# Queries' sum of squares in two rounded products, and the last denominators moved behind the second weight matrices

## The chip, the cores and the metric

One core of one Trainium2 chip runs the whole program. The metric is the device time of one execution in microseconds. The engines are TensorE (PE: matmuls and transposes; PEld: its weight loads), VectorE (DVE), ScalarE (ACT), GpSimd (POOL) and SyncE (SP), which issues the DMAs. Matrix results land in PSUM, in banks of 128 partitions x 512 floats; everything else lies in SBUF.

## The reference, cut to what matters

The block is a cross attention of latents on a context, then a self attention in fp8, then a gated attention, each with a residual. The change touches the first.

```python
# x (16, 64, 256), ctx (16, 1601, 128); Wq (256, 2048), Wk, Wv (128, 2048), Wo (2048, 256); 16 heads of 128
def rmsnorm(x, g, eps=EPS):
    var = jnp.mean(jnp.square(x), axis=-1, keepdims=True)
    return x * jax.lax.rsqrt(var + eps) * g
q = (hidden_states @ Wq).reshape(B, Sq, H, D)      # hidden_states = layernorm(x)
k = (encoder_hidden_states @ Wk).reshape(B, Skv, H, D)
v = (encoder_hidden_states @ Wv).reshape(B, Skv, H, D)
q = rmsnorm(q, gq); k = rmsnorm(k, gk)
scores = jnp.einsum('bqhd,bkhd->bhqk', q, k) * scale
out = jnp.einsum('bhqk,bkhd->bqhd', softmax(scores), v)
return out.reshape(B, Sq, H * D) @ Wo
```

## The kernel before

Products in float32 take several passes of TensorE. The kernel avoids most of them: it rounds an operand to a shorter float (type F32R, a "high" part, written by ScalarE), keeps the rest in a "low" part (a subtraction on VectorE or GpSimd), and adds two or three products of rounded parts in PSUM. Each engine has its own list of instructions, written out by hand; semaphores order them. `wait_ge(S.name, n)` holds an engine's queue until the counter has reached n, and `.then_inc` counts when an instruction is done.

**`queries`** (the first stage) computes the normed queries, multiplied by the keys' weights. There are 32 items, a head and one of two groups of 512 latents each. Every engine runs `step(n, m, o)` with m = n - 1 and o = n - 2, so three items are under way. For an item TensorE makes six rounded products into psK (L391, `Wq` times the normed latents), ScalarE squares the result (L459) and rounds it scaled into qgh (L468), VectorE makes the rest qgl (L551). For item m TensorE sums the squares over the 128 partitions: one float32 product with a matrix of ones into psS (L399). ScalarE takes the logarithm (L476), then for item o the exponential y (L464) and its square half (L473); VectorE refines the inverse root in two steps, scaled (L548) and root (L555, both operands in SBUF), and writes the queries from psO, times root (L560). psO comes from three more products (L406). psK, psS and psO have two banks each, square and y two buffers, qgh and qgl three. In items 4, 8, 12 and 16 TensorE also makes Gram matrices of the keys' weights, in items 17, 19, 21 and 23 it turns weights of a later stage, and at `GAIN_AT` and `GAIN_ALL_AT` it reduces a gain. `Wq` is loaded in four pieces; GpSimd makes their low parts wql (L311) and then sets `T.raw` to zero (L314), where three of the pieces lay. SP waits for that and loads the first two batches of the context there (`load_context`, L180, L181), and waits for them (L198) before the stage can end.

**`cross_attention`** runs over 8 pairs of batches, 26 tiles of context rows a pair, 13 a batch, and a pipelined step for each tile. TensorE: a transpose (L850), four key chunks (L808, L809), two halves of scores (L819), two halves of weighing (L828). VectorE: key products (L1238, L1249), the split cTl of the transposed context (L1277), scores scaled (L1260). ScalarE: sums, exponentials, roundings. GpSimd: the softmax sums c_acc and small root steps. A batch's softmax denominators are made while the next batch runs, in two halves of 512 columns. `SUMMED_AT = (0, 3)` gives the tile of the next batch in which TensorE makes each half's sum in the bank psM (L839, L840, in `denominators`); `LOG_AT = (1, 4)` and `INVERSE_AT = (2, 5)` are those of ScalarE's logarithm and exponential; `NEWTON_AT = (2, 5)` and `FULL_AT = (3, 6)` those of VectorE's `newton_start` (L1434, reads psM, counts dneg) and `newton_end` (L1439, two operands in SBUF, counts dfull); `NORM_AT = (5, 7)` that of GpSimd's scaling of the output (L1510). psM is one bank, so the second half's product must wait until the first half's sum has been read; it waits for dneg. In a step VectorE comes to the newton steps last, after `products`, `scale_scores` and `products_summed(i, x, 1)`; TensorE comes to `denominators` after key chunk 1 of the step. `batch_done(i, batch, 2, half)` is the count when `half` halves of this batch are done. The last batch's denominators lie in `end`, with a bank of their own (psT) for the second half.

**`end`** of `cross_attention` multiplies `Wv` and `Wo` of each head into one matrix (`turn` transposes, L888; `matrices`, L904; four heads at a time) and the weighted context with it (`product`, L922, in eight segments of four items). ScalarE and VectorE split the operands (`weighed_high` L1128, `weighed_low` L1320, `v_low` L1310), and again the order is written out by hand. Segments 2 and 3 and the last two need the second half of the latents, whose last batch is scaled by the last denominators.

Of the kernel before, what the change touches and what calls it, by code (L numbers as in the profile page):

```python
# [175 lines left out]
def load_context(nc, sp, T, dram, i, b, sems):  # L176
# [13 lines left out]
             "gram gramh graml zeroed context m8 m2 sel causal iota selb wgate wqkv turn turned gT gtop gall")  # L190
Q_SLOTS = 3
X_SLOTS = 2 * BANK // DIM
ITEM_SEMS = "q square qgh qgl total log y half newton root qw out"


def queries(nc, T, psum, dram):
    psT, psK, psS, psO, psM = psum
    with ExitStack() as ctx:  # L198
# [9 lines left out]
        wk, wq_last = T.queries[:, NPAIR - 1, :, :, :].rearrange("p b h q -> p (b h q)"), sb("wq", [P, WC, BANK])  # L208
# [5 lines left out]
        square, log, half = sb("square", [P, 2, BANK]), sb("log", [P, BANK]), sb("half", [P, BANK])  # L214
        y, scaled, root = sb("y", [P, 2, BANK]), sb("scaled", [P, BANK]), sb("root", [P, BANK])
# [15 lines left out]
        def wq(q):  # L231

            size = WC * BANK
            return wq_last[:, :, :] if q == KC - 1 else T.raw[:, q * size:(q + 1) * size].rearrange("p (k n) -> p k n", k=WC)
# [18 lines left out]
        GAIN_AT, GAIN_ALL_AT = 28, 30  # L253
# [10 lines left out]
        @block.sync  # L264
        def _(sp):
            sp.dma_start(T.xs[:, :, :], dram["x"].rearrange("b q c -> (b q) c").rearrange("(n p) c -> p n c", p=P)).then_inc(S.x, 16)
            for q, sem in enumerate(wq_there):
                sp.dma_start(wq(q), dram["L0_xattn_Wq"].rearrange("(k p) n -> p k n", p=P)[:, :, quad(q)]).then_inc(sem, 16)
# [6 lines left out]
            sp.wait_ge(S.zeroed, 1)  # L275
            for b in range(2):
                load_context(nc, sp, T, dram, 0, b, (S.context, S.context))
            sp.wait_ge(S.context, 64)

        @block.gpsimd  # L280
        def _(pool):
# [27 lines left out]
            for q in range(KC):  # L309
                pool.wait_ge(S.wqh, q + 1)  # L310
                nc.gpsimd.tensor_tensor(wql[:, :, quad(q)], wq(q), wqh[:, :, quad(q)].bitcast(F32), ALU.subtract).then_inc(S.wql, 1)  # L311

            pool.wait_ge(S.wql, KC)
            nc.gpsimd.memset(T.raw[:, :], 0.0).then_inc(S.zeroed, 1)  # L314

        @block.tensor
        def _(pe):
# [51 lines left out]
            def step(n, m, o):  # L369
# [12 lines left out]
                if n is not None:  # L382
                    h, g = items[n]
                    if h % HB == 0 and g == 0:
                        pe.wait_ge(S.wql, h // HB + 1)
# [26 lines left out]
        def _(act):  # L412
            nc.scalar.preload_act_table_set(LN_EXP)

            def wq_high(q):
                act.wait_ge(wq_there[q], 16)
                nc.scalar.activation(wqh[:, :, quad(q)], wq(q), ACT.Copy).then_inc(S.wqh, 1)
# [34 lines left out]
            act.wait_ge(S.made, 1)  # L452

            def step(n, m, o):
# [19 lines left out]
                if m is not None:  # L474
                    act.wait_ge(S.total, m + 1)
                    nc.scalar.activation(log[:, :], psS[:, m % 2, :], ACT.Ln, scale=1.0 / D, bias=T.eps[:, :]).then_inc(S.log, 1)  # L476
# [9 lines left out]
        def _(dve):  # L486
# [44 lines left out]

            def gram_low(q):
# [3 lines left out]
            def step(n, m, o):  # L536
# [7 lines left out]
                if o is not None:  # L544
                    dve.wait_ge(S.half, o + 1)
                    if o:
                        dve.wait_ge(S.root, o)
                    nc.vector.scalar_tensor_tensor(scaled[:, :], psS[:, o % 2, :], float(D * EPS), half[:, :], ALU.add, ALU.mult).then_inc(S.newton, 1)  # L548
# [4 lines left out]
                if o is not None:  # L553
                    dve.wait_ge(S.newton, o + 1)
                    nc.vector.scalar_tensor_tensor(root[:, :], scaled[:, :], 1.5, y[:, o % 2, :], ALU.subtract, ALU.mult).then_inc(S.root, 1)  # L555
                    dve.wait_ge(S.root, o + 1)
                    dve.wait_ge(S.qw, o + 1)
                    if o == GROUPS * (H - HB):
                        dve.wait_ge(S.turned, 2 * WC)
                    nc.vector.scalar_tensor_tensor(out(o), psO[:, o % 2, :].rearrange("p (m q) -> p m q", q=SQ), -1.0,  # L560
# [25 lines left out]
def cross_attention(nc, T, psum, dram):  # L586
    psT, psK, psS, psO, psM = psum
    with ExitStack() as ctx:
# [206 lines left out]
        def _(pe):  # L795
# [35 lines left out]
            def denominators(i, batch, half):  # L831
# [4 lines left out]
                if den_bank(i, batch, half) is psM_all:  # L836
                    pe.wait_ge(S.dneg, batch_done(i, batch, 2, half))
# [39 lines left out]
            def turn(q):  # L877
# [5 lines left out]
                if q >= 2:  # L883
                    pe.wait_ge(S.dneg, batch_done(LAST, 1, 2))
# [120 lines left out]
        def _(act):  # L1005
# [151 lines left out]
            def end(i, batch):  # L1157
                weighed_high(0)
                logarithms(i, batch, 0)
                weighed_high(1)  # L1160
                inverses(i, batch, 0)
                weighed_high(2)
                logarithms(i, batch, 1)
                weighed_high(3)
# [64 lines left out]
        def _(dve):  # L1229
# [150 lines left out]
            def end(i, batch):  # L1380
                weighed_low(0)
                newton_start(i, batch, 0)
                weighed_low(1)
                newton_end(i, batch, 0)
                weighed_low(2)
                newton_start(i, batch, 1)
                weighed_low(3)
                newton_end(i, batch, 1)
                product_low(1)
                next_segment(0)  # L1390
                wo_low(2)
                v_low(2)
                next_segment(1)
# [759 lines left out]
```

## Time and profile before

| | us |
|---|---|
| device time, median of 3 runs | 1481.54 (1479.16 to 1481.94) |
| the profiled execution, its own time | 1480.01 |
| its span (first to last instruction) | 1478.0 |
| TensorE busy | 1386.3 (94%) |
| VectorE busy | 1259.4 (85%) |
| ScalarE busy | 1202.5 (81%) |
| GpSimd busy | 982.6 (66%) |

`queries` runs from 22.7 us (its first product) to 139.5 us, the pipelined steps of `cross_attention` to 1237 us, its end to 1318 us, the two self attentions to the end. A busy time counts an instruction from start to end; matmuls follow each other before the one ahead has ended, so the distance between starts is what one costs. The granted clock is a share of TensorE's 2.4 GHz: 1.00, or 0.50 for 1.2 GHz.

### The profile page before, as it was taken

The page shows a single profiled execution, that of the slowest core. Times are in us where ns is not written, and L with a number is a line of the kernel's source. Part 1 is how long each engine was busy: PE and PEld are TensorE (multiplying, and loading weights), DVE is VectorE, ACT ScalarE, POOL GpSimd, SP SyncE. Part 2 cuts the span into 40 slices and gives each one's busy share as a digit, 9 for nine tenths or more (in the row PEclk, how much of TensorE's full clock was granted, in tenths as well). Part 3 has the DMA queues.
Part 4 walks back from the last instruction along what each step waited for, and adds up shares of the span by engine and source line. Part 5 has one row for each costly group of instructions (what it writes and reads, how often), then busy time and mean ns, then how long its engine had stood idle before and what let it go on. Part 6 is the DMA issues. An engine that isn't in the chain of part 4 may idle for free. (4 is left out here: it accounts for less than half of the span.)

```text
span 1478.0 us, 31543 instructions
## 1 busy us (share of the span) xinstructions
PE 1386.3 (94%) x5980; PEld 936.6 (63%) x5980; DVE 1259.4 (85%) x5006; ACT 1202.5 (81%) x4843; POOL 982.6 (66%) x1505
## 2 busy tenths in 40 slices
PE   5997999999999999999999999999999999966886
PEld 4664666666666666666666666666666666854554
DVE  6776888998989898889989898998998998756985
ACT  5886889898898989898988988898989887535763
POOL 4000788888989898889889898988888885010000
PEclk9998999999999999999999999999999999986998
DMA  4000000000000000000000000000000001000000
GB/s 143 38 1 1 1 2 24 4 21 16 10 23 1 24 1 23 2 23 2 23 13 13 23 1 25 1 23 2 23 1 27 22 30 64 1 1 1 8 7 16
DMA packets 9849, 25.30 MB, mean 17 GB/s; under 512 B 736, under 2 KB 6016, under 8 KB 9520
## 3 DMA queue, kind: packets, MB, share of 16 engines
q1 hardware_dynamic: 9648, 23.49, 4.4%
q14 instruction: 181, 1.48, 0.3%
q8 instruction: 20, 0.33, 0.1%
HBM read 22.44 MB, written 1.05 MB: 16 GB/s over the span
## 5 line engine op out<-in xcount | busy, mean ns | idle before, releaser
L1014 ACT ACTIVATE c_unused<-c_prod 124x128 f32<-124x128 f32 x1664 | 493.1, 298 | 83.6 <-DVE c_prod L1238 77.5
L1554 POOL TENSOR_TENSOR c_acc<-c_acc,c_prob 123x1024 f32<-123x1024 f32 (+1 forms) x192 | 461.9, 2406 | 23.9 <-ACT c_prob L1021 23.2
L1249 DVE CUSTOM_DVE_ANT_0 c_multiplied<-psK,c_c 124x128 f32<-124x128 f32 x1664 | 381.5, 285 | 57.0 <-PE psK L809 57.0
L808 PE MATMUL psK<-wkh,c_cTh 128*124 128x512 f32 x832 | 413.5, 497 | 10.9 <-DVE c_cTl L1277 9.2
L828 PE MATMUL psO<-c_prob,raw 123*128 123x512 f32 (+1 forms) x832 | 392.1, 594 | 0.0
L1238 DVE TENSOR_TENSOR c_prod<-psK,c_c 124x512 f32<-124x512 f32 x416 | 286.0, 688 | 53.4 <-PE psK L809 40.1
L809 PE MATMUL psK<-wkl,c_cTh 128*124 128x512 f32 x832 | 329.6, 396 | 0.0
L1014 ACT ACTIVATION_READ_ACCUMULATOR c_unused<-c_prod 124x1 f32 x1664 | 311.3, 187 | 0.0
L1260 DVE TENSOR_TENSOR c_prob<-psS,c_ss 124x512 f32<-124x512 f32 x416 | 265.7, 680 | 0.5 <-POOL c_ss L1537 0.5
L1021 ACT ACTIVATE c_prob<-c_prob,shift 124x1024 f32<-124x1024 f32 x208 | 236.6, 1137 | 0.4 <-DVE c_prob L1260 0.4
L808 PEld LDWEIGHTS psK<-wkh,c_cTh 128*124 128x124 f32 x832 | 154.2, 185 | 114.7 <-DVE c_ss L1249 47.5
L828 PEld LDWEIGHTS psO<-c_prob,raw 123*128 123x128 f32 (+1 forms) x832 | 142.0, 191 | 117.7 <-issue 99.4
L809 PEld LDWEIGHTS psK<-wkl,c_cTh 128*124 128x124 f32 x832 | 155.4, 187 | 69.4 <-issue 46.9
L819 PE MATMUL psS<-c_qwh,c_cTh 128*124 128x512 f32 x416 | 164.3, 395 | 0.0
L819 PE MATMUL psS<-c_qwh,c_cTl 128*124 128x512 f32 x416 | 164.0, 394 | 0.0
L819 PE MATMUL psS<-c_qwl,c_cTh 128*124 128x512 f32 x416 | 163.6, 393 | 0.0
L1448 POOL TENSOR_TENSOR c_low<-raw,c_ch 124x384 f32<-124x384 f32 x64 | 68.7, 1073 | 115.4 <-ACT c_ch L1050 115.4
L1249 DVE DVE_READ_ACCUMULATOR2_ANT c_ss<- 124x1 f32 x1664 | 137.4, 83 | 0.0
L819 PEld LDWEIGHTS psS<-c_qwl,c_cTh 128*124 128x124 f32 x416 | 76.8, 185 | 19.8 <-issue 0.2
L819 PEld LDWEIGHTS psS<-c_qwh,c_cTl 128*124 128x124 f32 x416 | 76.7, 184 | 19.8
L819 PEld LDWEIGHTS psS<-c_qwh,c_cTh 128*124 128x124 f32 x416 | 76.8, 185 | 19.5 <-issue 0.2
L1032 ACT ACTIVATE c_ss<-c_ss,eps 124x16 f32<-124x16 f32 x208 | 62.8, 302 | 23.1 <-DVE c_ss L1249 17.0
(314 smaller groups left out, 2165.2 us busy)
## 6 DMA issues: line engine op xcount, KB each, us to landing
raw<-in_ctx SPq DMA_DIRECT2D x16, 799.5 KB
raw<-in_L_xattn_Wq SPq DMA_DIRECT2D x3, 512.0 KB, 9.5
xs<-in_x SPq DMA_DIRECT2D x1, 1024.0 KB, 5.8
big<-in_L_xattn_Wk SPq DMA_DIRECT2D x1, 1024.0 KB, 8.7
c_prod<-in_L_xattn_Wo SPq DMA_DIRECT2D x1, 1024.0 KB, 5.3
out<-s_y SPq DMA_DIRECT2D x8, 128.0 KB, 1.7
big<-in_L_ffn_W_qkv SPq DMA_DIRECT2D x1, 768.0 KB, 12.5
raw<-in_L_xattn_Wv SPq DMA_DIRECT2D x1, 768.0 KB, 4.1
```

The source lines that it names most:

```text
L808: nc.tensor.matmul(psK[0:ROWS, c % 2, :], cTh[:, slot, :], T.wkh[:, cols], start=True, stop=False)
L809: nc.tensor.matmul(psK[0:ROWS, c % 2, :], cTh[:, slot, :], T.wkl[:, cols], start=False, stop=True).then_inc((S.k0, S.k1, S.k2, S.k3)[c], 1)
L819: last = nc.tensor.matmul(psS[0:ROWS, half, :], x[:, slot, :], w[:, b, cols], start=(n == 0), stop=(n == 2))
L828: nc.tensor.matmul(psO[:, half, :], raw[0:rows, b, tile, :], prob[0:rows, probs(v), half * BANK:(half + 1) * BANK], start=(tile == 0), sto ...
L1014: last = nc.scalar.activation(unused[:, j, :], prod[:, k % 2, c // 2, j * CD:(j + 1) * CD], ACT.Copy, accum_out=ss[:, k % 2, 0, h:h + 1])
L1021: nc.scalar.activation(prob[:, probs(e), :], prob[:, probs(e), :], ACT.Exp, bias=T.shift[0:ROWS, :]).then_inc(S.expd, 1)
L1032: nc.scalar.activation(ss[:, r % 2, 2, :], ss[:, r % 2, 0, :], ACT.Ln, scale=1.0 / D, bias=T.eps[0:ROWS, :]).then_inc(R.log, 1)
L1238: nc.vector.tensor_tensor(prod[:, k % 2, c // 2, :].rearrange("p (h c) -> p h c", c=CD), psK[0:ROWS, 0, :].rearrange("p (h c) -> p h c", c ...
L1249: last = nc.vector.tensor_tensor_reduce(multiplied[:, j, :], psK[0:ROWS, 1, cols], c2[:, k % NT, :], 1.0, 0.0, ALU.mult, ALU.add, ss[:, k ...
L1260: nc.vector.tensor_tensor(prob[:, probs(s), cols].rearrange("p (h q) -> p h q", q=SQ), psS[0:ROWS, half, :].rearrange("p (h q) -> p h q", ...
L1448: nc.gpsimd.tensor_tensor(low[:, PIECES[piece], :], raw[:, batch % 2, PIECES[piece], :], ch[:, PIECES[piece], :].bitcast(F32), ALU.subtrac ...
L1554: nc.gpsimd.tensor_tensor(acc[0:rows, batch % 2, :], acc[0:rows, batch % 2, :], prob[0:rows, probs(s), :], ALU.add).then_inc(S.acc, 1)
```

## The change

In `queries`, GpSimd copies the square into a high part squareh and makes a low part squarel, and TensorE sums both with rounded ones (`onesr`, made by ScalarE), two products in place of one float32 product. The sum is made for item o, no longer for item m; ScalarE's logarithm moves with it, to the head of the step. VectorE writes `scaled` in place into psS, and qgl stands ahead of it, no longer between scaled and root. The low parts of the third and fourth piece of `Wq` are made by VectorE ahead of its steps. `T.raw` is set to zero in four parts, behind the low parts of items 20 to 23. Each piece of `Wq` is loaded by two DMAs, the fourth into a free part of the queries' tile. The gain's steps move from items 28 and 30 to 25 and 28.

In `cross_attention`, `newton_start` writes in place into the denominators' bank, `newton_end` reads it there, and the products that need the bank wait for dfull. In `end`, the second weight matrices and the first segment stand ahead of the denominators on TensorE, ScalarE and VectorE. The tables of tiles stay as they are.

```diff
@@ queries, gpsimd
-            for q in range(KC):
-                pool.wait_ge(S.wqh, q + 1)
-                nc.gpsimd.tensor_tensor(wql[:, :, quad(q)], wq(q), wqh[:, :, quad(q)].bitcast(F32), ALU.subtract).then_inc(S.wql, 1)
-            pool.wait_ge(S.wql, KC)
-            nc.gpsimd.memset(T.raw[:, :], 0.0).then_inc(S.zeroed, 1)
+            nc.gpsimd.memset(blank[:, :], 0.0).then_inc(S.blank, 1)
...
+            def step(n, m, o):
+                if m is None:
+                    return
+                pool.wait_ge(S.square, m + 1)
+                if m >= 2:
+                    pool.wait_ge(S.total, m - 1)
+                nc.gpsimd.tensor_tensor(squareh[:, m % 2, :], square[:, m % 2, :], blank[:, :].broadcast_to([P, BANK]), ALU.add).then_inc(S.squareh, 1)
+                pool.wait_ge(S.squareh, m + 1)
+                nc.gpsimd.tensor_tensor(squarel[:, m % 2, :], square[:, m % 2, :], squareh[:, m % 2, :].bitcast(F32), ALU.subtract).then_inc(S.squarel, 1)
+                if m in ZERO_AT:
...
+                    nc.gpsimd.memset(T.raw[:, ZERO[ZERO_AT.index(m)]], 0.0).then_inc(S.zeroed, 1)
@@ queries, tensor
-                if m is not None:
-                    pe.wait_ge(S.square, m + 1)
-                    if m >= 2:
-                        pe.wait_ge(S.newton, m - 1)
-                    nc.tensor.matmul(psS[:, m % 2, :], T.ones[:, :], square[:, m % 2, :], start=True, stop=True).then_inc(S.total, 1)
                 if o is not None:
+                    pe.wait_ge(S.squarel, o + 1)
+                    if o >= 2:
+                        pe.wait_ge(S.root, o - 1)
+                    nc.tensor.matmul(psS[:, o % 2, :], onesr[:, :], squareh[:, o % 2, :], start=True, stop=False)
+                    nc.tensor.matmul(psS[:, o % 2, :], onesr[:, :], squarel[:, o % 2, :], start=False, stop=True).then_inc(S.total, 1)
@@ queries, scalar
             def step(n, m, o):
+                if o is not None:
+                    act.wait_ge(S.total, o + 1)
+                    nc.scalar.activation(log[:, :], psS[:, o % 2, :], ACT.Ln, scale=1.0 / D, bias=T.eps[:, :]).then_inc(S.log, 1)
                 if n is not None:
                     act.wait_ge(S.q, n + 1)
                     if n >= 2:
-                        act.wait_ge(S.total, n - 1)
+                        act.wait_ge(S.squarel, n - 1)
@@ queries, vector: after qgl
+                    nc.vector.scalar_tensor_tensor(psS[:, o % 2, :], psS[:, o % 2, :], float(D * EPS), half[:, :], ALU.add, ALU.mult).then_inc(S.newton, 1)
                     dve.wait_ge(S.newton, o + 1)
-                    nc.vector.scalar_tensor_tensor(root[:, :], scaled[:, :], 1.5, y[:, o % 2, :], ALU.subtract, ALU.mult).then_inc(S.root, 1)
+                    nc.vector.scalar_tensor_tensor(root[:, :], psS[:, o % 2, :], 1.5, y[:, o % 2, :], ALU.subtract, ALU.mult).then_inc(S.root, 1)
@@ cross_attention, tensor: denominators
                 if den_bank(i, batch, half) is psM_all:
-                    pe.wait_ge(S.dneg, batch_done(i, batch, 2, half))
+                    pe.wait_ge(S.dfull, batch_done(i, batch, 2, half))
@@ cross_attention, tensor: end
-                denominators(i, batch, 0)
-                pe.wait_ge(W.vTl, 2)
-                denominators(i, batch, 1)
                 matrices(1)
                 segment(0)
+                denominators(i, batch, 0)
+                denominators(i, batch, 1)
+                segment(1)
                 turn(2)
                 turn(3)
-                segment(1)
                 segment(2)
@@ cross_attention, scalar: end (vector alike)
-                weighed_high(0)
-                logarithms(i, batch, 0)
...
-                inverses(i, batch, 1)
+                for n in range(HB):
+                    weighed_high(n)
                 product_high(1)
                 next_segment(0)
+                for half in range(2):
+                    logarithms(i, batch, half)
+                    inverses(i, batch, half)
                 wo_high(2)
+                next_segment(1)
                 v_high(2)
-                next_segment(1)
@@ cross_attention, vector
-                nc.vector.scalar_tensor_tensor(den[:, 2, :], den_bank(i, batch, half), -1.0, den[:, 1, :], ALU.mult, ALU.mult).then_inc(S.dneg, 1)
+                nc.vector.scalar_tensor_tensor(den_bank(i, batch, half), den_bank(i, batch, half), -1.0, den[:, 1, :], ALU.mult, ALU.mult).then_inc(S.dneg, 1)
...
-                nc.vector.scalar_tensor_tensor(den[:, 3, :], den[:, 2, :], 2.0, den[:, 1, :], ALU.add, ALU.mult).then_inc(S.dfull, 1)
+                nc.vector.scalar_tensor_tensor(den[:, 3, :], den_bank(i, batch, half), 2.0, den[:, 1, :], ALU.add, ALU.mult).then_inc(S.dfull, 1)
```

## Rows read from the trace of the kernel before

**Rows 1.** Busy time by stretch: PE, PEld, DVE, ACT, POOL, then clock, DMA share, GB/s.

```profile
160.00:1237.00 1077.00, 1070.02 (x3997) 709.57 (x3995) 967.32 (x4394) 954.76 (x4311) 945.81 (x1453) 1.00 0.04 15
...
1241.00:1248.00 7.00, 6.95 (x24) 6.07 (x25) 6.13 (x10) 4.85 (x10) 2.38 (x2) 0.55 0.00 0
```

**Rows 2.** Instructions in order of time, TensorE, one item of the queries: start, us, line.

```profile
125.55 0.51 PE L391 MATMUL psK<-q_xTh,q_wqh 128*128 128x512 f32 x1
...
127.06 1.02 PE L399 MATMUL psS<-q_square,ones 128*128 128x512 f32 x2
...
128.62 0.39 PE L391 MATMUL psK<-q_xTh,q_wqh 128*128 128x512 f32 x1
...
128.85 0.39 PE L391 MATMUL psK<-q_xTh,q_wql 128*128 128x512 f32 x1
```

**Rows 3.** Instructions in order of time, ScalarE, the squares of the queries' stage.

```profile
120.08 0.60 ACT L459 ACTIVATE q_square<-psK 128x512 f32<-128x512 f32 x1 [0.34 <-PE psK L391]
...
123.27 0.60 ACT L459 ACTIVATE q_square<-psK 128x512 f32<-128x512 f32 x1 [0.40 <-PE psK L391]
...
130.23 0.60 ACT L459 ACTIVATE q_square<-psK 128x512 f32<-128x512 f32 x1 [0.17 <-PE psK L391]
```

**Rows 4.** Instructions in order of time, VectorE, late in the queries' stage.

```profile
119.19 0.69 DVE L548 SCALAR_TENSOR_TENSOR q_scaled<-psS,q_half 128x512 f32<-128x512 f32 x1 [0.62 <-ACT q_half L473]
...
122.33 0.69 DVE L548 SCALAR_TENSOR_TENSOR q_scaled<-psS,q_half 128x512 f32<-128x512 f32 x1 [0.46 <-ACT q_half L473]
...
135.06 0.68 DVE L548 SCALAR_TENSOR_TENSOR q_scaled<-psS,q_half 128x512 f32<-128x512 f32 x1
...
137.11 0.68 DVE L548 SCALAR_TENSOR_TENSOR q_scaled<-psS,q_half 128x512 f32<-128x512 f32 x1
...
139.34 0.15 DVE L569 TENSOR_SCALAR shift<-q_limit 128x1 f32<-128x1 f32 x1
```

**Rows 5.** Groups by line, GpSimd: count, busy us, mean ns, idle before and releaser.

```profile
L1464 POOL TENSOR_TENSOR c_qwl<-big,c_qwh 128x512 fp32r<-128x512 f32 x32 | 40.9, 1278 | 2.9 <-ACT c_qwh L1042 2.9
...
L1551 POOL TENSOR_TENSOR c_acc<-c_prob,zero 124x1024 f32<-124x1024 f32 x16 | 30.3, 1893 | 7.9 <-ACT c_prob L1021 7.9
...
L314 POOL MEMSET raw<- 128x3328 f32 x1 | 2.9, 2877 | 0.1
```

**Rows 6.** SyncE's queue: the last context load's issue, and its wait for the loads.

```profile
32.46 3.30 SPq L181 DMA_DIRECT2D raw<-in_ctx  x1
...
SPq L198 <- DMA raw<-in_ctx: 19.5, 1, 19.5
```

**Rows 7.** Order of time, cross attention: second denominators and `newton_end`, first and last pair.

```profile
248.69 0.40 PE L839 MATMUL psM<-c_sum_high,c_unit 124*128 124x512 f32 x1
...
250.39 0.69 DVE L1439 SCALAR_TENSOR_TENSOR c_den<-c_den 128x512 f32<-128x512 f32 x1
...
1198.36 0.40 PE L839 MATMUL psM<-c_sum_high,c_unit 124*128 124x512 f32 x1
...
1200.06 0.69 DVE L1439 SCALAR_TENSOR_TENSOR c_den<-c_den 128x512 f32<-128x512 f32 x1
```

**Rows 8.** Waits of TensorE, 160 to 1220 us: total, times, longest.

```profile
PE psK L808 <- DVE c_cTl L1277: 6.7, 18, 0.9
```

**Rows 9.** Order of time, TensorE: matmuls behind gaps, with the gap in brackets.

```profile
22.73 0.77 PE L391 MATMUL psK<-q_xTh,q_wqh 128*128 128x512 f32 x1 [2.97 <-issue]
...
23.30 0.63 PE L391 MATMUL psK<-q_xTh,q_wql 128*128 128x512 f32 x1
...
23.72 0.63 PE L391 MATMUL psK<-q_xTl,q_wqh 128*128 128x512 f32 x1
...
133.31 1.10 PE L399 MATMUL psS<-q_square,ones 128*128 128x512 f32 x2 [1.17 <-DVE q_scaled L548]
...
1239.72 0.50 PE L839 MATMUL psM<-c_sum_high,c_unit 124*128 124x512 f32 x1 [2.50 <-POOL c_turned_low L1543]
```

**Rows 10.** Order of time, VectorE, at the end of the cross attention.

```profile
1238.46 0.68 DVE L1310 TENSOR_TENSOR c_turned_low<-psT,c_turned 128x512 fp32r<-128x512 f32 x1
```

More of the change, by code:

```diff
@@ L189 @@
 PREP_SEMS = ("x gains wk wq0 wq1 wq2 wq3 consts gprod made stats moments centred lnT lnTh lnTl wkT wkTh wkTl wqh wql "
-             "gram gramh graml zeroed context m8 m2 sel causal iota selb wgate wqkv turn turned gT gtop gall")
+             "wql0 onesr blank gram gramh graml zeroed context m8 m2 sel causal iota selb wgate wqkv turn turned gT gtop gall")
 Q_SLOTS = 3
 X_SLOTS = 2 * BANK // DIM
-ITEM_SEMS = "q square qgh qgl total log y half newton root qw out"
+ITEM_SEMS = "q square squareh squarel qgh qgl total log y half newton root qw out"
 def queries(nc, T, psum, dram):
@@ L213, in queries @@
         xTh, xTl = sb("xTh", [P, WC, NPAIR * P], F32R), sb("xTl", [P, WC, NPAIR * P], F32R)
-        square, log, half = sb("square", [P, 2, BANK]), sb("log", [P, BANK]), sb("half", [P, BANK])
-        y, scaled, root = sb("y", [P, 2, BANK]), sb("scaled", [P, BANK]), sb("root", [P, BANK])
+        with ExitStack() as shared:
+            square = shared.enter_context(nc.sbuf_tensor("q_square", [P, 2, BANK], F32))
+        squarel = sb("squarel", [P, 2, BANK], F32R)
+        squareh, onesr, blank = sb("squareh", [P, 2, BANK], F32R), sb("onesr", [P, P], F32R), sb("blank", [P, 1])
+        log, half = sb("log", [P, BANK]), sb("half", [P, BANK])
+        y, root = sb("y", [P, 2, BANK]), sb("root", [P, BANK])
         qgh, qgl = sb("qgh", [P, Q_SLOTS, BANK], F32R), sb("qgl", [P, Q_SLOTS, BANK], F32R)
@@ L252, in queries @@
         gain_row, gain_all = psM[0:1, 0:P], psM[:, P:P + 1]
-        GAIN_AT, GAIN_ALL_AT = 28, 30
+        GAIN_AT, GAIN_ALL_AT = 25, 28
+        ZERO_AT = (20, 21, 22, 23)
+        ZERO = [slice(2 * NT * CD * n // 4, 2 * NT * CD * (n + 1) // 4) for n in range(4)]
         def out(n):
@@ L267, in _ @@
             for q, sem in enumerate(wq_there):
-                sp.dma_start(wq(q), dram["L0_xattn_Wq"].rearrange("(k p) n -> p k n", p=P)[:, :, quad(q)]).then_inc(sem, 16)
+                for k in range(WC):
+                    sp.dma_start(wq(q)[:, k, :, :], halved(dram["L0_xattn_Wq"].rearrange("(k p) n -> p k n", p=P)[:, :, quad(q)])[:, k, :, :]).then_inc(sem, 16)
                 if q == 0:
@@ L274, in _ @@
             sp.dma_start(wgate, dram["L0_ffn_W_gate"]).then_inc(S.wgate, 16)
-            sp.wait_ge(S.zeroed, 1)
+            sp.wait_ge(S.zeroed, len(ZERO))
             for b in range(2):
@@ L383, in step @@
                     h, g = items[n]
-                    if h % HB == 0 and g == 0:
-                        pe.wait_ge(S.wql, h // HB + 1)
+                    if h == 0 and g == 0:
+                        pe.wait_ge(S.wql0, 1)
+                    elif h == HB and g == 0:
+                        pe.wait_ge(S.wql0, 2)
+                    elif h % HB == 0 and g == 0:
+                        pe.wait_ge(S.wql, h // HB - 1)
                     if n >= 2:
@@ L530, in _ @@
             nc.vector.tensor_copy(T.identb[:, :], T.ident[:, :]).then_inc(S.made, 1)
+            for q in range(2, KC):
+                dve.wait_ge(S.wqh, q + 1)
+                nc.vector.tensor_tensor(halved(wql[:, :, quad(q)]), wq(q), halved(wqh[:, :, quad(q)]).bitcast(F32), ALU.subtract).then_inc(S.wql, 1)
             def gram_low(q):
@@ L543, in step @@
                         nc.vector.tensor_reduce(gtop[:, :], gain_row, AX.X, ALU.max, apply_absolute_value=True).then_inc(S.gtop, 1)
[L544 to L548, printed above, removed]
                 if n is not None:
@@ L553, in step @@
                 if o is not None:
+                    dve.wait_ge(S.half, o + 1)
+                    if o:
+                        dve.wait_ge(S.root, o)
+                    nc.vector.scalar_tensor_tensor(psS[:, o % 2, :], psS[:, o % 2, :], float(D * EPS), half[:, :], ALU.add, ALU.mult).then_inc(S.newton, 1)
                     dve.wait_ge(S.newton, o + 1)
-                    nc.vector.scalar_tensor_tensor(root[:, :], scaled[:, :], 1.5, y[:, o % 2, :], ALU.subtract, ALU.mult).then_inc(S.root, 1)
+                    nc.vector.scalar_tensor_tensor(root[:, :], psS[:, o % 2, :], 1.5, y[:, o % 2, :], ALU.subtract, ALU.mult).then_inc(S.root, 1)
                     dve.wait_ge(S.root, o + 1)
@@ L883, in turn @@
                 if q >= 2:
-                    pe.wait_ge(S.dneg, batch_done(LAST, 1, 2))
+                    pe.wait_ge(S.dfull, batch_done(LAST, 1, 2))
                 if q == 3:
@@ L1380, in end @@
             def end(i, batch):
[L1381 to L1388, printed above, removed]
+                for n in range(HB):
+                    weighed_low(n)
                 product_low(1)
                 next_segment(0)
+                for half in range(2):
+                    newton_start(i, batch, half)
+                    newton_end(i, batch, half)
                 wo_low(2)
+                next_segment(1)
                 v_low(2)
-                next_segment(1)
                 wo_low(3)
```

33 lines of the change are left out of this document (21 added, 12 removed).

## The prediction, made before the change was run

> **What bounds the kernel now.** I read the busy time by stretch first, because the share over the whole span mixes stages; then single instructions in order of time, stage by stage; last the waits of one engine. Between 160 and 1237 us TensorE is busy 1070.0 of 1077.0 us at granted clock 1.00, VectorE 967.3 and ScalarE 954.8 [rows 1]. Nothing on TensorE is spare there: each microsecond that it is made to wait lengthens the kernel, while the others have about a tenth free.
>
> Then the queries' stage, one item at a time. Two first products L391 start 3.07 us apart, with 9 rounded matmuls 0.23 us apart and the unrounded sum L399 between them [rows 2]: 9 x 0.23 = 2.10, which leaves 0.97 us for L399 and its hand-over. ScalarE starts its squares 3.19 us apart and sat idle 0.40 us of it waiting for TensorE: its work is 2.79 us an item [rows 3]. VectorE starts its newton steps 3.14 us apart with 0.46 us idle: 2.68 us [rows 4]. So TensorE bounds this stage too, but two engines stand close behind.
>
> Last the cross attention around the denominators, the order of instructions in time. The second half's denominators (L839) start at 248.69; VectorE's `newton_end` of the first half (L1439) starts at 250.39 and takes 0.69 [rows 7]. I followed this pair through all 15 batches in which both halves lie in the pipelined steps: the distance is 1.70 us each time, the last pair included [rows 7].
>
> **The change part by part.** Sum of squares. Two rounded products cost 2 x 0.23 = 0.47 in place of 0.97 us, so TensorE needs 2.57 us an item, 0.50 less. The stage does not get all of it. VectorE now runs scaled, root and out behind each other with no other work between: three such steps take 2.05 us at the end of the stage (137.11 - 135.06), and qgl's step is the rest of the item, 2.68 - 2.05 = 0.63 at least, so 2.7 us. ScalarE stays at up to 2.79. I take 2.75 us an item: 32 x (3.07 - 2.75) = 10.2. In the eight items with Gram matrices or turned weights TensorE has extra work and keeps more of its 0.50: another 8 x 0.1. Bounds: 16 us (the whole 0.50 each) and 4 us, if the longer chain square, two GpSimd parts, sum, logarithm adds a few tenths per item.
>
> GpSimd's parts. The high part is an addition of a broadcast zero; such an addition over 1024 columns takes 1.89, so 0.95 for 512; the low part is like L1464, 1.28 [rows 5]. 2.3 us with hand-overs against a period of 2.75: hidden. The four parts of the memset add 2.9 / 4 = 0.7 us in items 20 to 23, where GpSimd then needs 3.0; I charge 0.5 us in all. VectorE's sums in PSUM in place instead of SBUF: no row shows VectorE writing PSUM. The steps that read it take 0.68 to 0.69 us, one that read SBUF alone can't be much shorter [rows 4]; between -0.05 and 0.1 us on the step, which is inside the bounds above, and I take 0, the nearest row's own duration.
>
> End of the stage. Before, 9.3 us pass from the last square at 130.23 to 139.49 [rows 3, 4]. After: square 0.6, GpSimd 0.95 + 1.28 + 0.2, sums 0.5, then logarithm, exponential and square on ScalarE at 0.7 each with hand-overs, three steps of VectorE 2.05 and the limit 0.3 make 8.0, so 1 us less.
>
> The context load moves behind the memset's last part. It took from about 31.5 to 55.3: its last issue ended at 35.76 and SP waited 19.5 us more, 23.8 in all [rows 6]. Now it starts after square 0.6, both parts 2.4, the memset's part 0.7 and what GpSimd has fallen behind, 0.8: 4.5 us after the square of item 23 begins, so it ends 28.3 behind that; the stage ends 8 x 2.75 + 8.0 = 30.0 behind it. Hidden with 1.7 us to spare; once that is gone, each late microsecond is lost whole (rival E). The split weight loads only issue four more DMAs ahead of loads that are queued anyway, and the two low parts moved to VectorE fall where it waited for the first product: 0, between a gain of 0.5 and a loss of 1 us, the width of a low part.
>
> Denominators in every batch. `newton_start` now writes into the PSUM bank, so the second half's product waits for dfull, `newton_end` of the first half, and no longer for dneg. The tables that place the steps are not changed. `denominators(half 1)` and `newton_end(half 0)` lie in the same step, and VectorE comes to it only after products, two scalings and four sums that this step's TensorE work has just fed. So TensorE arrives at 248.69 and can go at 250.39 + 0.69 = 251.08; with 0.1 us to start again it waits 2.5 us, 15 times: 37.5 us [rows 7]. Behind the waiting product on its queue stand the third key chunk, the next transpose and the weighing, and VectorE's next products need that chunk. Given back: `newton_end` no longer reads two operands in SBUF beside GpSimd; TensorE's waits for c_cTl in the whole loop are 6.7 us in 18, the longest 0.9 [rows 8]. I take back a third, 2.4, since only the short ones stand behind a `newton_end`; between 0 and 6.7. Not waiting at all would need VectorE 2.4 us earlier, and it has no such idle in that step.
>
> The clock. TensorE idle 2.97 us (to 22.73) was followed by matmuls 0.42 us apart, the 1.2 GHz level; idle 2.50 us (to 1239.72) by a granted clock of 0.55 from 1241 to 1248; idle 1.17 us (to 133.31) by no fall [rows 9, 1]. 0.55 over 7 us is 6.3 us at the lower level, and there matmuls come 0.42 instead of 0.23 us apart, so 6.3 x (1 - 0.23 / 0.42) = 2.9 us of work are lost. A gap of 2.5 us stands nearest the second row, but that one had a shorter wait close behind it; I take two falls in three: 10 x 2.9 = 29. Bounds 0 and 15 x 2.9 = 44.
>
> The Trainium skill, "TensorE: Matmul & The Clock Gate", section "Why this matters for your kernels", advises against idle gaps above about 3 us between bursts. By that these gaps would cost nothing beyond themselves; the row at 1239.72 speaks against it. It is rival B.
>
> The end. The last denominators no longer hold up TensorE, which waited 2.50 us there [rows 9]; the second weight matrices can start when c_turned_low is there, at 1238.46 + 0.68 = 1239.14 [rows 10], 0.6 us earlier, and a second, shorter wait goes or turns into one for the first low part. One clock fall of 2.9 may go as well. I take 1.5 us, between 0 and 4; what the denominators release (norm, turned weights) is needed only a segment later: 4 heads x 6 products x 0.23 = 5.5 us of TensorE's work against log, inverse, two steps and the scaling of GpSimd, 0.7 x 4 + 1.3 = 4.1.
>
> Sum on the profiled execution: 1478.0 - 11.0 + 0.5 - 1.0 + 37.5 - 2.4 + 29.0 - 1.5 = 1529.1 us span, 1531.1 with the 2.0 us around it (1480.01 against 1478.0). That run lies 1.5 us below the median of 1481.54: forecast 1532.6, rounded 1532.
>
> **Rivals.** A is the forecast: the wait is real and the clock falls behind most gaps. 1532, own range 1516 to 1547.
>
> B, the wait is real and the clock holds (0 to 3 falls): for it, 1.17 us had no effect and the 2.50 row was not one lone gap; against it, the 2.97 and 2.50 rows. 1532 - 29 = 1503.
>
> C, the wait falls the clock every time, and the queries' stage gains little since the three engines' chains interlock: 1532 + 15 + 7 = 1554. For it: ScalarE and VectorE had just 0.40 and 0.46 us idle per item. Against it: gaps at 15 different times should not all strike alike.
>
> D, the other side: VectorE reaches `newton_end` before TensorE needs the bank, so no wait. Its place is the fourth step of the next batch; it decides from the point where TensorE waits less than (11.0 - 0.5 + 1.0 + 2.4 + 1.5) / 15 = 1.0 us per batch, that is if VectorE ran 1.5 us earlier there. Then only the gains stand: 1480 + 1.5 - 11 + 0.5 - 1 - 2.4 - 1.5 = 1466. For it: VectorE is 10% idle in the loop [rows 1]. Against it: 15 pairs at the same 1.70 us, and a `newton_end` that needs sums of this very step.
>
> E, the context load outlasts the stage by some 3 us: 1535. Against it, the 1.7 us to spare; for it, any further delay of GpSimd's queue.
>
> **How the numbers follow.** A 0.57, B 0.22, C 0.13, D 0.05, E 0.03 (with A's sign). The time is A's, 1532. The range reaches to B's middle and above A's own end: 1500 to 1550, leaving out D, the low side of B and most of C. A measurement of this kernel can tell about 0.2% (3 us) from no change. Faster comes from D, 0.04; same 0.02; slower 0.94.
>
> **What would show it.** In the changed kernel's trace: the second half's first denominator product, with about 2.4 us idle before it, released by VectorE's den step, 15 times; granted clock below 1.00 for about 7 us behind most of them; the unrounded sum gone and items about 2.75 us apart, with ScalarE nearly full; GpSimd busy from 26 us on; SP's wait for the context ending ahead of the stage's last VectorE step. I am wrong if no such idle shows in the loop, or if TensorE catches it up within the batch (the batches of the loop then last as long as before).

## The result, and the profile after

The changed kernel takes 1520.48 us (median of 4 runs, 1517.1 to 1523.58), the one before 1481.74 (1479.16 to 1482.07) beside it: ratio 1.0265 [1.0238, 1.0292], slower. The forecast was 1532. The profiled execution's span went from 1478.0 to 1520.2 us.

The page of the changed kernel: busy time with the share of the span, and the clock and TensorE in 40 slices.

```profile
span 1520.2 us, 31654 instructions
...
PE 1394.3 (92%) x5980; PEld 943.1 (62%) x5980; DVE 1256.2 (83%) x5008; ACT 1202.4 (79%) x4844; POOL 1044.9 (69%) x1571
...
PE   5996999999999999999999999999999999975886
...
PEclk9997999999999999999999999999999999996998
```

The shares of TensorE, VectorE and ScalarE fell (from 94, 85 and 81%), and the slices point at no single place. So the loss may lie in small pieces, and the waits name them. In the changed kernel L882 and L883 are the denominators' products in psM (L839 and L840 before), L1470 is `newton_start`, L1475 `newton_end`, L851 and L852 the key chunks. TensorE's waits (us in total, times, longest):

```profile
PE psM L882 <- DVE c_den L1475: 35.3, 15, 2.4
...
PE psK L851 <- DVE c_cTl L1316: 6.6, 8, 1.9
```

The order of time around the third of the 15 (start, us), VectorE's step ahead and TensorE's work behind it, to be read against [rows 7]:

```profile
380.68 0.69 DVE L1475 SCALAR_TENSOR_TENSOR c_den<-psM,c_den 128x512 f32<-128x512 f32 x1
...
381.51 0.63 PE L882 MATMUL psM<-c_sum_high,c_unit 124*128 124x512 f32 x1 [2.37 <-DVE c_den L1475]
381.94 0.63 PE L883 MATMUL psM<-c_turned_low,c_unit 124*128 124x512 f32 x1
382.37 0.63 PE L851 MATMUL psK<-wkh,c_cTh 128*124 128x512 f32 x1
382.80 0.63 PE L852 MATMUL psK<-wkl,c_cTh 128*124 128x512 f32 x1
```

TensorE stands for 2.37 us, until `newton_end` has ended, and then its matmuls are 0.43 us apart in place of 0.23. Busy time by stretch (columns as in [rows 1]), behind the first of the gaps, then before, in and behind the fall at the second, then behind the third:

```profile
239.70:243.20 3.50, 3.49 (x12) 2.21 (x13) 0.88 (x2) 2.17 (x9) 0.95 (x2) 1.00 0.00 0
...
309.00:309.98 0.98, 0.80 (x4) 0.69 (x5) 0.04 (x1) 0.00 (x0) 0.26 (x2) 1.00 0.00 0
309.98:313.39 3.41, 3.41 (x8) 1.66 (x6) 0.88 (x2) 2.48 (x10) 1.20 (x1) 0.50 0.00 0
313.39:314.40 1.01, 1.01 (x5) 0.63 (x5) 0.05 (x1) 0.00 (x0) 1.01 (x1) 1.00 0.00 0
...
381.50:385.00 3.50, 3.49 (x7) 2.10 (x8) 0.88 (x2) 1.33 (x3) 0.19 (x1) 0.52 0.00 0
```

Behind the first gap 12 matmuls run in 3.5 us at 1.00, behind the third 7 at 0.52. Of the 15 gaps all but the first are followed by one stretch of 3.41 us at the lower level, 1.2 GHz, and then the clock is back. By an estimate from the distances of the matmuls one such stretch costs 3.41 x (1 - 0.23 / 0.43) = 1.59 us. It shows in the batches: from the first half's sums of one batch to the next went 67.31 us before (233.03 to 300.34) and 69.50 after (221.49 to 290.99), with a gap and no fall: +2.2. The next batch, with gap and fall, went from 68.49 (300.34 to 368.83) to 72.34 (290.99 to 363.33): +3.85, which is 1.66 more. These first halves' sums in the kernel before, in order of time, then in the changed one:

```profile
233.03 0.40 PE L839 MATMUL psM<-c_sum_high,c_unit 124*128 124x512 f32 x1
...
300.34 0.40 PE L839 MATMUL psM<-c_sum_high,c_unit 124*128 124x512 f32 x1
...
368.83 0.39 PE L839 MATMUL psM<-c_sum_high,c_unit 124*128 124x512 f32 x1
```

```profile
221.49 0.39 PE L882 MATMUL psM<-c_sum_high,c_unit 124*128 124x512 f32 x1
...
290.99 0.40 PE L882 MATMUL psM<-c_sum_high,c_unit 124*128 124x512 f32 x1
...
363.33 0.39 PE L882 MATMUL psM<-c_sum_high,c_unit 124*128 124x512 f32 x1
```

The queries' stage gained what was forecast. In order of time in the changed kernel, ScalarE's squares (3.19 us apart in [rows 3]), and VectorE's last step of the stage (139.34 in [rows 4]):

```profile
110.86 0.59 ACT L500 ACTIVATE q_square<-psK 128x512 f32<-128x512 f32 x1
...
113.53 0.61 ACT L500 ACTIVATE q_square<-psK 128x512 f32<-128x512 f32 x1
...
116.19 0.64 ACT L500 ACTIVATE q_square<-psK 128x512 f32<-128x512 f32 x1
...
118.96 0.59 ACT L500 ACTIVATE q_square<-psK 128x512 f32<-128x512 f32 x1
...
127.98 0.15 DVE L612 TENSOR_SCALAR shift<-q_limit 128x1 f32<-128x1 f32 x1
```

Sum of the two traces, stage by stage. The queries' stage ends at 128.13 in place of 139.49: -11.4. From there to the start of the last weighing (1235.35 before, 1279.10 after) the pipelined steps took 55.1 us more. From the last weighing to the last segment's last product (1294.44 and 1336.48) the end took 1.7 less. Together +42.0, and the spans differ by 42.2.

### The profile page after: what moved, and what is told of

Read it like the earlier page. It is cut to its first block and busy times, and to the rows that moved or that the text cites. A ratio compares the mean times of both kernels' runs of the same rounds, so it can differ in the third digit from the quotient of the medians.

```text
span 1520.2 us, 31654 instructions
## 1 busy us (share of the span) xinstructions
PE 1394.3 (92%) x5980; PEld 943.1 (62%) x5980; DVE 1256.2 (83%) x5008; ACT 1202.4 (79%) x4844; POOL 1044.9 (69%) x1571
## 5 line engine op out<-in xcount | busy, mean ns | idle before, releaser
L851 PE MATMUL psK<-wkh,c_cTh 128*124 128x512 f32 x832 | 415.2, 499 | 8.4 <-DVE c_cTl L1316 6.6
L871 PE MATMUL psO<-c_prob,raw 123*128 123x512 f32 (+1 forms) x832 | 409.2, 616 | 0.0
L852 PE MATMUL psK<-wkl,c_cTh 128*124 128x512 f32 x832 | 332.1, 399 | 0.0
L871 PEld LDWEIGHTS psO<-c_prob,raw 123*128 123x128 f32 (+1 forms) x832 | 148.7, 199 | 126.6 <-issue 109.3
L851 PEld LDWEIGHTS psK<-wkh,c_cTh 128*124 128x124 f32 x832 | 156.1, 188 | 108.9 <-DVE c_ss L1288 47.5
L852 PEld LDWEIGHTS psK<-wkl,c_cTh 128*124 128x124 f32 x832 | 156.3, 188 | 71.1 <-issue 47.6
L1102 ACT ACTIVATE c_cTh<-psT 128x124 fp32r<-128x124 f32 x208 | 53.1, 255 | 54.0 <-PE psT L893 45.4
```

The lines of the kernel that those rows point to most:

```text
L851: nc.tensor.matmul(psK[0:ROWS, c % 2, :], cTh[:, slot, :], T.wkh[:, cols], start=True, stop=False)
L852: nc.tensor.matmul(psK[0:ROWS, c % 2, :], cTh[:, slot, :], T.wkl[:, cols], start=False, stop=True).then_inc((S.k0, S.k1, S.k2, S.k3)[c], 1)
L871: nc.tensor.matmul(psO[:, half, :], raw[0:rows, b, tile, :], prob[0:rows, probs(v), half * BANK:(half + 1) * BANK], start=(tile == 0), sto ...
L1102: nc.scalar.activation(cTh[:, CT_SLOT[x % TP], :], psT[:, 0:ROWS], ACT.Copy).then_inc(S.cth, 1)
```

## The experiments

Theory W, mine: the wait for dfull (`newton_end` of the first half) stops TensorE 2.4 us in 15 batches, and the clock falls behind these gaps. Rivals: R, the loss comes from the new arrangement of the stages; P, the step that writes its own PSUM bank is what costs; the clock's part is something else; the queries' gain is not a gain. A ratio below stands against runs of the kernel before that were taken beside each experiment (medians 1480.96 to 1482.47).

**1. The denominators undone**, the rest of the change kept.

```diff
-                    pe.wait_ge(S.dfull, batch_done(i, batch, 2, half))
+                    pe.wait_ge(S.dneg, batch_done(i, batch, 2, half))
...
-                nc.vector.scalar_tensor_tensor(den_bank(i, batch, half), den_bank(i, batch, half), -1.0, den[:, 1, :], ALU.mult, ALU.mult).then_inc(S.dneg, 1)
+                nc.vector.scalar_tensor_tensor(den[:, 2, :], den_bank(i, batch, half), -1.0, den[:, 1, :], ALU.mult, ALU.mult).then_inc(S.dneg, 1)
...
-                nc.vector.scalar_tensor_tensor(den[:, 3, :], den_bank(i, batch, half), 2.0, den[:, 1, :], ALU.add, ALU.mult).then_inc(S.dfull, 1)
+                nc.vector.scalar_tensor_tensor(den[:, 3, :], den[:, 2, :], 2.0, den[:, 1, :], ALU.add, ALU.mult).then_inc(S.dfull, 1)
```

> The changed kernel with the denominators' part undone: newton_start writes to SBUF again, the bank is waited for by dneg. Theory W (TensorE waits 2.35 us for newton_end in 15 batches and the clock falls behind 14 of them): the loop is as before, so 1481.7 less the 11.4 us of the queries' stage and the 1.7 us of the end, 1468.6. Rival R (the loss is not the wait, but comes from the stages' new arrangement, a shifted loop or the later context load): it stays above 1500.

Measured: 1468.03 (1466.65 to 1474.95), ratio 0.9916 [0.9898, 0.9934], span 1467.0. The loss parts cleanly from the rest of the change, which gains 13 us, while the denominators cost 52.

**2. The denominators alone**: the same lines the other way, in the kernel before.

```diff
-                    pe.wait_ge(S.dneg, batch_done(i, batch, 2, half))
+                    pe.wait_ge(S.dfull, batch_done(i, batch, 2, half))
...
```

> The kernel before with the denominators' part alone. W: 1481.7 + 55 = 1537, with 15 waits of 2.35 us. R: within 5 us of 1482.

Measured: 1535.39 (1530.7 to 1540.82), ratio 1.0354 [1.0336, 1.0371]. TensorE's wait for the bank is 35.4 us, 15 times, and the granted clock fell behind all 15.

**3. The wait alone**: the kernel before with nothing but S.dneg turned into S.dfull at the two waits; the steps still write SBUF.

```diff
-                    pe.wait_ge(S.dneg, batch_done(i, batch, 2, half))
+                    pe.wait_ge(S.dfull, batch_done(i, batch, 2, half))
...
-                    pe.wait_ge(S.dneg, batch_done(LAST, 1, 2))
+                    pe.wait_ge(S.dfull, batch_done(LAST, 1, 2))
```

> The kernel before with only the wait changed, dneg to dfull; newton_start writes to SBUF as before. W: the wait alone costs it all, 1481.7 + 55, and up to 3 more since newton_end still reads two operands in SBUF beside GpSimd: 1537 to 1540. Rival P (VectorE's write into the PSUM bank is what costs): within 3 us of 1482.

Measured: 1537.17 (1534.3 to 1540.44), ratio 1.0375 [1.0354, 1.0396]. Its waits of TensorE:

```profile
PE psM L839 <- DVE c_den L1439: 35.3, 15, 2.4
```

As slow as experiment 2, with PSUM not written by VectorE at all, so rival P falls. The two times agree partly by chance, though: here the clock fell behind 11 of the 15 gaps, not behind all. Behind the second gap, then behind the third, columns as in [rows 1]:

```profile
319.90:323.40 3.50, 3.50 (x8) 2.03 (x9) 0.89 (x2) 1.61 (x5) 0.65 (x3) 0.54 0.00 0
392.80:396.30 3.50, 3.50 (x12) 2.20 (x13) 0.89 (x3) 2.19 (x9) 1.23 (x3) 1.00 0.00 0
```

That prices a fall directly. From the first half's sums of one batch to the next, batches at the same place in a pair took 69.8 us with a gap and no fall (231.86 to 301.63) and 71.4 with both (517.01 to 588.43): 1.65 us, near the estimate of 1.59. In experiment 2 such batches with gap and fall took 70.9 to 71.0. There `newton_end` of the second half reads PSUM and takes 0.69 us, here it has both operands in SBUF and takes 1.16 to 1.20. So the write in place costs nothing, and reading PSUM gives about 0.4 us a batch back; four falls fewer hide it here.

**4. The queries' part alone**: the kernel before with the changed `queries`.

> The kernel before with the queries' part alone. W: 1481.7 - 11.4 = 1470.3. A rival within it, that the stage's gain is partly lost again in the first tiles or at the context load: 1473 or more.

Measured: 1469.99 (1468.19 to 1472.26), ratio 0.9921 [0.9908, 0.9935], 11.0 us less than the 1480.96 beside it and 11.7 less than 1481.7. The -11.4 of the trace lies between.

**5. The new order at the end alone**: before's queries and denominators, after's end.

> The kernel before with the new order of the end alone. W: 1481.7 - 1.7 = 1480.0, or down to 1477 if the clock's fall at 1241 goes as well; a rival, that the end gained only because the loop ended at another phase of the clock: within 1 us of 1481.7.

Measured: 1479.0 (1477.58 to 1486.06), ratio 0.9991 [0.9978, 1.0004]. Inconclusive: the interval holds both no gain and one of 3 us. Its own trace, of a run of 1485.7, has the end of the cross attention 1.0 us longer than before (60.08 for 59.09). Experiments 1 and 4 differ by the order at the end alone: 1468.03 for the new one, 1469.99 for the old, with ranges that overlap (1466.65 to 1474.95, 1468.19 to 1472.26). The 1.7 us of the traces are not shown by times.

**6. newton_end sooner**: both halves' second step in the tile of the first one, so that the bank is free early.

```diff
-LOG_AT, INVERSE_AT, NEWTON_AT, FULL_AT, NORM_AT = (1, 4), (2, 5), (2, 5), (3, 6), (5, 7)
+LOG_AT, INVERSE_AT, NEWTON_AT, FULL_AT, NORM_AT = (1, 4), (2, 5), (2, 5), (2, 5), (5, 7)
```

> The changed kernel with newton_end one tile sooner, in the same step as newton_start (FULL_AT 2 and 5 in place of 3 and 6), still in PSUM. W: dfull is there before TensorE comes, no wait, no fall of the clock, and the 2 us given back by the shorter newton_end stay: 1466.5, below the kernel with that part undone. P: the PSUM writes are unchanged, above 1500.

Measured: 1485.37 (1481.3 to 1489.57), ratio 1.0029 [1.0016, 1.0042]. The wait is gone and no clock falls, 35 us better than the change, but 19 more than I expected. TensorE's waits in it:

```profile
PE psK L851 <- DVE c_cTl L1316: 20.4, 38, 1.9
```

And the order of time around a pair of VectorE's steps:

```profile
303.05 0.69 DVE L1470 SCALAR_TENSOR_TENSOR psM<-psM,c_den 128x512 f32<-128x512 f32 x1
303.78 0.69 DVE L1475 SCALAR_TENSOR_TENSOR c_den<-psM,c_den 128x512 f32<-128x512 f32 x1
...
305.31 0.49 PE L851 MATMUL psK<-wkh,c_cTh 128*124 128x512 f32 x1 [0.42 <-DVE c_cTl L1316]
```

Two steps of 0.69 us now stand behind one another on VectorE, and what TensorE wants next, the low part of the turned context, comes 0.42 us late. I had counted the moved step at nothing; in tile 2 it has a neighbour that TensorE's next operand waits behind. Experiment 10 tests it.

**7. The second half later**: all steps of the second half one tile on, so that its sums meet a bank already free.

```diff
-SUM_HIGH_AT, SUM_LOW_AT, SUMMED_AT = (-1, 0), (-1, 0), (0, 3)
-LOG_AT, INVERSE_AT, NEWTON_AT, FULL_AT, NORM_AT = (1, 4), (2, 5), (2, 5), (3, 6), (5, 7)
+SUM_HIGH_AT, SUM_LOW_AT, SUMMED_AT = (-1, 0), (-1, 0), (0, 4)
+LOG_AT, INVERSE_AT, NEWTON_AT, FULL_AT, NORM_AT = (1, 5), (2, 6), (2, 6), (3, 7), (5, 8)
```

> The changed kernel with the second half of the denominators one tile later (tiles 4, 5, 6, 7, 8 in place of 3, 4, 5, 6, 7). W: no wait either, 1466 to 1468. If two dependent steps of VectorE at one place (as in the other kernel) cost anything, this one is the faster of the two by 1 to 2 us.

Measured: 1461.71 (1460.78 to 1467.31), ratio 0.988 [0.9859, 0.9901]: 59 us ahead of the change, 20 ahead of the kernel before, and 4 to 6 below what I expected, which experiment 9 takes up. Order of time in it:

```profile
374.01 0.69 DVE L1475 SCALAR_TENSOR_TENSOR c_den<-psM,c_den 128x512 f32<-128x512 f32 x1
...
377.39 0.40 PE L882 MATMUL psM<-c_sum_high,c_unit 124*128 124x512 f32 x1
```

The bank is free at 374.70 and wanted at 377.39: the same wait stands in the code and costs nothing, with 2.7 us to spare.

**8. A shorter gap**: in VectorE's step `newton_end` comes ahead of the products' sums of the same step.

```diff
+                for batch, half in sums_at(w, FULL_AT):
+                    newton_end(i, batch, half)
                 if x is not None:
                     products_summed(i, x, 1)
                 for batch, half in sums_at(w, NEWTON_AT):
                     newton_start(i, batch, half)
-                for batch, half in sums_at(w, FULL_AT):
-                    newton_end(i, batch, half)
```

> The changed kernel with newton_end ahead of products_summed(x, 1) in VectorE's step: the wait shrinks by the four sums, 0.84 us, to some 1.5 us. If the clock does not fall behind gaps of this length: 1466.5 + 15 x 1.6 = 1490. If it falls behind each as before: 1490 + 15 x 1.5 = 1513. Under P the time does not move from 1520.

Measured: 1492.7 (1490.42 to 1494.17), ratio 1.0077 [1.0059, 1.0095]. TensorE's wait for the bank in it:

```profile
PE psM L882 <- DVE c_den L1475: 22.6, 15, 1.5
```

One such gap with what follows, in order of time:

```profile
378.51 0.47 PE L882 MATMUL psM<-c_sum_high,c_unit 124*128 124x512 f32 x1 [1.52 <-DVE c_den L1475]
378.82 0.40 PE L883 MATMUL psM<-c_turned_low,c_unit 124*128 124x512 f32 x1
379.05 0.40 PE L851 MATMUL psK<-wkh,c_cTh 128*124 128x512 f32 x1
```

And the busy time of the stretch that holds all 15, columns as in [rows 1]:

```profile
160.00:1250.00 1090.00, 1062.66 (x3957) 701.15 (x3955) 953.65 (x4348) 947.38 (x4266) 927.99 (x1436) 1.00 0.04 15
```

Behind a gap of 1.52 us the matmuls are 0.31 and then 0.23 us apart. The gaps shrank by 35.3 - 22.6 = 12.7 us and the span by 1520.2 - 1490.1 = 30.1. That leaves 17.4 for the clock, where 14 x 1.59 = 22.3 were to come back. Of the 4.9 missing, 2.1 lie outside the loop (0.7 in the queries' stage, 1.1 in the end, 0.3 behind it) and 2.8 in it, which stay unplaced.

**9. The second half later, steps back in SBUF**: experiment 7 with experiment 1's lines.

> The kernel with every second half's sum, logarithm, inverse, both denominator steps and normalisation one tile later (1461.7 us, span 1459.0), but with the denominator steps back in SBUF and the sums waiting for the first step, as before. It tells apart why that kernel is 6 us ahead of the one with the denominators undone (1468.0, span 1467.0). Theory P, the step that reads PSUM gives it: 30 times 0.28 us (0.968 with both operands in SBUF, 0.686 with one in PSUM) off VectorE, and the time is about 1467. Theory T, the place of the second half gives it (6 tiles between the halves in place of 4 to 5, so two busy VectorE steps don't meet): 1461 to 1463. Mean of the second step is 0.95 to 0.97 by P, and by T it falls towards 0.7, because GpSimd is at something else in that tile.

Measured: 1462.23 (1459.79 to 1463.22), ratio 0.986 [0.9844, 0.9877]. The same as experiment 7: its 6 us over experiment 1 come from the place of the steps, and there reading PSUM adds nothing. VectorE's `newton_end` by line, 160 to 1230 us, the first from experiment 1 and the second from this one:

```profile
L1475 DVE SCALAR_TENSOR_TENSOR c_den<-c_den 128x512 f32<-128x512 f32 x30 | 29.0, 968 | 0.0
```

```profile
L1475 DVE SCALAR_TENSOR_TENSOR c_den<-c_den 128x512 f32<-128x512 f32 x30 | 20.6, 687 | 0.0
```

One instruction, one shape: 685 to 1319 ns by instance in experiment 1 and 685 to 698 here. The 14 long ones, 1249 ns and more, are all of the second half. The one at 391.11 shares 0.72 us with a GpSimd subtraction on SBUF tiles (L1492, `c_c<-raw,c_low`); the short ones share 0.16 us at most with it, and here the second half's share none. That is 0.57 us a batch less on VectorE, and the batches became 0.5 shorter (67.39 to 66.85 for the first). Experiment 3 against 2 has the same gain by the other way, the operand in PSUM.

**10. The first half sooner alone.**

```diff
-LOG_AT, INVERSE_AT, NEWTON_AT, FULL_AT, NORM_AT = (1, 4), (2, 5), (2, 5), (3, 6), (5, 7)
+LOG_AT, INVERSE_AT, NEWTON_AT, FULL_AT, NORM_AT = (1, 4), (2, 5), (2, 5), (2, 6), (5, 7)
```

> The changed kernel with the second denominator step of the first half alone in the tile of its first step (tiles 2 and 6 in place of 3 and 6). The kernel with both halves so took 1485.4 us and its TensorE waited for c_cTl 36 times, 17.8 us in the loop. Theory D, two denominator steps of 0.69 us behind one another make VectorE some 0.42 us late for TensorE's next key chunk: the 15 pairs left cost 15 times 0.42 = 6.3 us, and the time is 1485.4 less 6.3 and less up to 2, so 1476 to 1480. Rival N, the second half's step there waited for the first half's normalisation on GpSimd: with it at tile 6 the whole loss is gone, 1462 to 1468. No wait for the denominators' bank by either.

Measured: 1474.55 (1471.32 to 1478.12), ratio 0.9942 [0.9923, 0.996]: about half-way from experiment 6 (1485.4) towards 1462 to 1468, 1.5 us below the 1476 to 1480 of theory D. TensorE waits for c_cTl 21 times instead of 36 between 160 and 1230 us, 11.6 us instead of 17.8: the 15 waits that are gone make 6.2. The other 4.6 of the 10.8 us are not placed. Rival N, by which all of it should have gone, falls, and 6.5 us over experiment 1 (1468.0) remain.

## Why the prediction was right

**Where the bound lies.** Right: what TensorE waited came through to the end (35.3 us of waits and 22.3 of lower clock in a loop that grew by 55.1). The loop is the only stage that grew.

**The queries' stage.** Forecast -11.0 + 0.5 for the items and -1.0 for the tail; it was -11.3 (last square 130.23 to 118.96) and -0.1 (9.26 to 9.17 us behind it). The sum of -11.5 held by errors that cancel. Plain items mostly came 2.65 to 2.83 us apart, 2.67 at the most regular place (113.53 - 110.86) and not 2.75: ScalarE needed less than the 2.79 that I had allowed it. By my formula that alone would be 32 x (3.07 - 2.67) = 12.8. But the item behind one with Gram matrices took as long as before, 3.15 us then (52.45 to 55.60) and 3.14 now; this I had missed. ScalarE's squares of such an item and the one ahead of it, changed kernel:

```profile
50.31 0.59 ACT L500 ACTIVATE q_square<-psK 128x512 f32<-128x512 f32 x1
...
53.45 0.62 ACT L500 ACTIVATE q_square<-psK 128x512 f32<-128x512 f32 x1
```

The tail gained nothing, and this step failed by a wait that I hadn't seen. TensorE in order of time in the changed kernel:

```profile
122.95 0.47 PE L436 MATMUL psS<-q_squareh,q_onesr 128*128 128x512 f32 x1 [1.05 <-DVE q_root L596]
```

The last sum was ready on GpSimd at 120.75 + 1.29 = 122.04, but its bank, one of two, held the item two before until VectorE's root step had read it at 122.12 + 0.69 = 122.81: scaling in place keeps the bank until that step. GpSimd's high part took 1.04 us, not 0.95.

**The context load.** Right: SyncE issued it from 101.02 to 103.76 and waited 20.6 us, so it landed near 124.4, 3.7 us ahead of the stage's end (1.7 forecast). Rival E didn't happen.

**The wait.** Right in place, cause and size: 15 times 2.34 to 2.37, 35.3 us for 37.5. Experiment 3 shows the cause. Given back, 2.4 forecast: the loop's 55.1 falls 2.5 short of 35.3 + 22.3. This is a remainder and not a measurement. Experiment 3 speaks for the reason given, the shorter `newton_end`: with it in SBUF nothing comes back, its loop grew by 55.7 for 35.3 + 11 x 1.59 = 52.8. In TensorE's waits for c_cTl, from which the 2.4 were worked out, it can't be read: between 160 and 1230 us they fell from 6.7 to 4.1 in the changed kernel and to 4.6 in experiment 3 alike.

**The clock.** Right that it falls, the size was off. Forecast: 10 falls of 2.9 us, 29.0. Measured: 14 falls, each 3.41 us long and not 6.3, worth 1.59, 22.3 in all. Two errors of opposite sign. The length was read off a row where a second wait stood close behind the gap ([rows 1, 9]); the stretches behind lone gaps are half as long, and whether the second wait made that one longer is not tested. The count is not fixed by the gap's length: the same gaps gave 15 falls in experiment 2 and 11 in experiment 3, and what decides which gap is spared stays open. Had the clock held, the forecast would have been 1503, rival B. The Trainium skill ("TensorE: Matmul & The Clock Gate", "Why this matters for your kernels") advises against idle gaps above about 3 us. The trace disagrees with that figure: gaps of 2.34 to 2.37 us were followed by the lower level 14 times in 15. Gaps of 1.50 to 1.52 us were not, in experiment 8, so what the rule warns of is real here, and only its figure is too high. Of the 11.5 us between forecast and result 6.7 are this term and 2.2 the wait. Most of the rest is no term of the kernel: I had put the median 3.5 us above the span, and it came 0.3 above it.

**The end.** Forecast -1.5, -1.7 in the trace, and this was luck. I had the waits shrink; they grew from 3.1 us (2.50 and 0.59) to 4.0. TensorE's waits from the last weighing to the last segment, changed kernel:

```profile
PE psK L947 <- DVE c_turned_low L1349: 2.0, 1, 2.0
PE psO L965 <- DVE c_split L1359: 1.3, 1, 1.3
PE psS L965 <- DVE c_split L1359: 0.7, 1, 0.7
```

What gained was the clock. Before, it stood at the lower level for 6.83 us there, in the changed kernel for none of the end (busy time by stretch, before and then changed):

```profile
1240.45:1247.28 6.83, 6.24 (x22) 5.49 (x22) 5.96 (x9) 4.76 (x9) 2.12 (x3) 0.50 0.00 0
```

```profile
1279.10:1336.48 57.38, 53.40 (x258) 43.72 (x256) 45.46 (x71) 33.54 (x57) 10.89 (x9) 1.00 0.06 19
```

Experiment 5's trace has the new order with 6.83 us at the lower level, and there the end is 1.0 us longer than before. So no run shows that the order gains anything apart from the clock.

With the measured terms in the forecast's own sum: 1478.0 - 11.4 + 35.3 - 2.5 + 22.3 - 1.7 = 1520.0 for a span of 1520.2. As the 2.5 is the loop's remainder, this shows that no other stage moved and does not test the split within the loop. B fell with the 14 falls in the changed kernel's trace, D with the first of the waits, and C was right in the number of falls only.

## What to carry to other kernels

When a result is to stay in the bank that the next product fills, the producer waits for the last reader instead of the copy: compare, in the trace of before, when the last reader ends and when the bank is wanted, and if they cross, move the second user to a later step in the same change (here 59 us between two placements of the same arithmetic). A gap on a full TensorE costs more than itself once it is long enough for the clock to fall (here 2.35 us in 40 cases of 45, 1.5 us in none of 15), so shortening it can pay more than its length. Moving a step "earlier" is free only where its new neighbours leave room for it.

## What the runs showed of the hardware

- TensorE's granted clock behind gaps of 2.34 to 2.37 us in an otherwise full stretch: 3.41 us at the 1.2 GHz level behind 14 of 15 in the changed kernel, 15 of 15 in experiment 2 and 11 of 15 in experiment 3, each worth about 1.6 us. Behind 15 gaps of 1.50 to 1.52 us it stayed at 2.4 GHz (experiment 8). In the changed kernel the lower level came 0.15 to 1.48 us after TensorE's start behind the gap; in experiment 2 it came up to 0.31 us before that start.
- A gap of 1.97 or 1.98 us at the end of the cross attention, with shorter waits behind it, was followed by a fall in experiments 1, 5, 6, 7, 8 and 9, and not in experiment 10; nor was the changed kernel's of 1.96.
- VectorE writing its PSUM operand in place took 694 ns (128x512), and 685 with an SBUF result (L1470 in the changed kernel and in experiment 1): no difference that matters.
- VectorE with both operands in SBUF: 0.69 us, or 1.25 to 1.32 in the same program where it met a GpSimd subtraction on SBUF tiles for 0.70 to 0.77 us (experiment 1); with one operand in PSUM it stayed at 0.68 to 0.70.
